# A graph and expert network on one core: the attention's ring of gathered blocks gets 32 slots in place of 25, over the place of the last stage's weights

## What is computed

```python
x = x + L0_gnn(layernorm(x))     # sum over edges of (x @ W[rel])[src] * weight, 16 relations
x = x + L0_ffn(layernorm(x))     # 16 experts, 2 for each node
x = x + L1_gnn(layernorm(x))     # two layers of graph attention, 8 heads of 32
x = x + L1_ffn(layernorm(x))     # a shared MLP and 4 gated experts

def gat_conv(x, src, dst, W, a_src, a_dst, b):
    h = (x @ W).reshape(N, HEADS, HEAD_DIM)
    alpha_s = jnp.einsum('nhc,hc->nh', h, a_src)
    alpha_d = jnp.einsum('nhc,hc->nh', h, a_dst)
    e = alpha_s[src] + alpha_d[dst]
    e = jnp.where(e > 0, e, NEG_SLOPE * e)
    m = jax.ops.segment_max(e, dst, num_segments=N)
    ex = jnp.exp(e - m[dst])
    denom = jax.ops.segment_sum(ex, dst, num_segments=N)
    alpha = ex / (denom[dst] + 1e-16)
    out = jax.ops.segment_sum(h[src] * alpha[:, :, None], dst, num_segments=N)
    return out.reshape(N, HEADS * HEAD_DIM) + b
```

## Time and profile before

| what | value |
| --- | --- |
| three runs | 3178.21, 3187.8, 3189.51 us |
| their median | 3187.8 us |
| the profiled execution's own time | 3155.48 us |
| its span in the profile | 3153.7 us |
| busy in it: PE, DVE, POOL, ACT | 62%, 49%, 44%, 29% |
| gathers of the attention, L1539 | 784, mean 1000 ns |

### The profile page before, as it was taken

One profiled execution on the slowest core, in us unless ns is written; L12 is line 12 of the kernel. 1 busy time (PEld: TensorE's weight loads), 2 busy tenths in 40 slices (PEclk: granted clock), 3 DMA queues, 4 the chain that ended last, 5 costly groups with the idle time before them and its releaser, 6 DMA issues.

```text
span 3153.7 us, 37574 instructions
## 1 busy us (share of the span) xinstructions
PE 1954.5 (62%) x10213; PEld 1541.1 (49%) x10213; DVE 1545.1 (49%) x4921; ACT 920.9 (29%) x2031; POOL 1402.8 (44%) x1413
## 2 busy tenths in 40 slices
PE   8998444354457999733554665564355465556599
PEld 6887233243337999622443443443244343344377
DVE  4200123233376555634564664675355555556753
ACT  5444667672013444320111111113011111111432
POOL 1100666666602344245555555513555555552143
PEclk9999677666778999876677666787677767776799
DMA  6544566564338999744344344313343443442000
GB/s 229 199 190 198 178 194 198 186 208 131 90 84 274 352 351 352 236 151 121 101 130 125 107 126 123 115 56 112 107 124 118 121 122 117 119 122 79 1 14 28
DMA packets 206433, 472.17 MB, mean 150 GB/s; under 512 B 33180, under 2 KB 99958, under 8 KB 199762
## 3 DMA queue, kind: packets, MB, share of 16 engines
q0 software_dynamic: 63424, 179.09, 20.0%
q1 hardware_dynamic: 111986, 188.65, 16.8%
q10 hardware_dynamic: 30816, 101.99, 9.1%
HBM read 365.49 MB, written 104.92 MB: 149 GB/s over the span
## 4 chain that ended last, share of the span: by engine, by line
PE 29%; another core or an unknown queue 29%; DVE 26%; issue 10%; DVEq 3%; DMA 2%; ACT 1%; POOL 1%; SPq 0%; ACTq 0%; POOLq 0%
PE banks L470 9%; PE banks L1332 7%; DVE arena L1737 3%; DVE arena L1821 3%; DVE arena L891 3%; PE banks L1344 3%; DVE X L900 2%; DVE arena L1786 2%; DVEq L761 2%; DVEq L764 1%; PE banks L1498 1%; PE banks L877 1%; DVE xn L1749 1%; PE banks L2240 1%
## 5 line engine op out<-in xcount | busy, mean ns | idle before, releaser
L1539 POOL DMA_INDIRECT arena<-ht,srcT x784 | 784.2, 1000 | 678.4 <-DVE arena L1821 382.1
L1648 PE MATMUL banks<-arena,XT 128*128 128x264 f32 x884 | 385.0, 527 | 281.1 <-DVE arena L1821 193.9
L849 POOL DMA_INDIRECT arena<-tr,idx1T x392 | 376.7, 961 | 362.0 <-DMA tr<-arena 175.2
L877 PE MATMUL banks<-arena 128*128 x884 | 259.9, 456 | 326.2 <-DVE arena L891 261.2
L877 PEld LDWEIGHTS banks<-arena 128*128 128x128 f32 x884 | 196.9, 231 | 389.3 <-issue 357.2
L1648 PEld LDWEIGHTS banks<-arena,XT 128*128 128x128 f32 x884 | 208.6, 255 | 347.5 <-DVE arena L1821 204.8
L1649 PE MATMUL banks<-arena,XT 128*128 128x264 f32 x884 | 352.6, 489 | 0.0
L1821 DVE TENSOR_TENSOR arena<-arena,nrmT 128x528 f32<-128x528 f32 x442 | 309.7, 703 | 20.3 <-issue 12.7
L900 DVE TENSOR_TENSOR X<-X,banks 128x256 f32 x221 | 91.8, 415 | 397.1 <-remote 368.9
L470 PE MATMUL banks<-parts 128*128 128x512 f32 x1200 | 281.0, 394 | 0.0
L1737 DVE TENSOR_TENSOR arena<-arena,banks 128x264 f32 x442 | 189.0, 428 | 136.2 <-remote 113.3
(11 more groups left out here) (381 smaller groups left out, 3268.1 us busy)
## 6 DMA issues: line engine op xcount, KB each, us to landing
arena<-in_L_ffn_w_dram SPq DMA_DIRECT2D x192, 512.0 KB
tr<-arena SPq DMA_DIRECT2D x50, 1024.0 KB, 3.9
XT<-otd ACTq DMA_DIRECT2D x52, 512.0 KB
arena<-ohd ACTq DMA_DIRECT2D x52, 512.0 KB
arena<-dld ACTq DMA_DIRECT2D x28, 512.0 KB
otd<-arena ACTq DMA_DIRECT2D x28, 512.0 KB
ohd<-arena ACTq DMA_DIRECT2D x28, 512.0 KB
arena<-ht,srcT POOLq DMA_INDIRECT x784
```

Source lines behind the costliest of these rows:

```text
L849: pool.indirect_dma_start(Gr[:, o:o + D], None, TR, bass.IndirectOffsetOnAxis(ap=idx1T[:, q:q + 1], axis=0)).then_inc(d_g[b % NG], 16)
L877: mm = ten.matmul(B[n][:, 0:D], OHr[:, n, h, :], Gr[:, h * D:][:, bass.ds(o, D)], start=(h == 0), stop=(h == 1))
L1539: pool.indirect_dma_start(Gall[:, o:o + ROW], None, HT[L], bass.IndirectOffsetOnAxis(ap=srcT[:, q:q + 1], axis=0)).then_inc(d_g[b % NG], 16)
L1648: ten.matmul(B[n][:, 0:MSG], OH[b][:, 2 * j, :], WG[:, j, 0, :], start=True, stop=False)
```

## The change

`RG` becomes 32 and the ring takes the place in which the last stage's large weights lay: these now overlap the ring's upper slots (`raw_at` is at the end of the region `parts2`), and only the small ones (biases, `B5`) keep a place at the top, over that of the first layer's weights. The table `given` starts at block 0 in place of block 3, and `NEAR` becomes 16. The 14 loads and the 4 behind them go to the end of the second attention layer: SyncE waits until all chunks but the last are weighed (`LAST_OF_RING`), and GpSimd clears the two tiles there in place of VectorE. `O`, `O2` and `hst` lie elsewhere in the arena than before; what reads and writes them is the same.

```diff
@@ -45,7 +45,7 @@
 HALF = 16
 NX = 3
 RB = 40
-RG = 25
+RG = 32
 GIVEN0 = (4 - RG) % 4
 KTH = 4096
 WHOLE = 12582912.0
@@ -823,7 +823,7 @@
 
         ld_ok = sem("ld_ok")
         landed = ten.alloc_register("landed")
-        NEAR = 20
+        NEAR = 16
         begun, starts = pool.alloc_register("begun"), [pool.alloc_register(f"start{i}") for i in range(16)]
 
         def pool_gather():
@@ -912,12 +912,20 @@
 
 
 
-        LATER = ARENA - 5600
+        LATER = ARENA - 1872
         top[0] = LATER
         wx2 = [take(2 * 272).rearrange("p (k c) -> p k c", k=2) for _ in range(2)]
         bb2 = [take(D) for _ in range(2)]
         tad = take((NS + CH) * 8)
-        raw_at = top[0]
+        top[0] = LATER
+        gB = take(4)
+        sb1 = take(2)
+        sb2 = take(1)
+        eb1 = take(4)
+        eb2 = take(2)
+        B5 = take(D)
+        assert top[0] <= LATER + 2 * 272
+        raw_at = top[0] = PARTS2_AT + PARTS2
         sW1 = take(2 * D).rearrange("p (k c) -> p k c", k=2)
         sW2 = take(2 * P).rearrange("p (k c) -> p k c", k=2)
         sW3 = take(D)
@@ -926,12 +934,6 @@
         eW3 = take(2 * D).rearrange("p (q c) -> p q c", q=2)
         gW = take(2 * 4).rearrange("p (k c) -> p k c", k=2)
         raw_end = top[0]
-        gB = take(4)
-        sb1 = take(2)
-        sb2 = take(1)
-        eb1 = take(4)
-        eb2 = take(2)
-        B5 = take(D)
 
         def by_tile(n, dt=F32, t=NT):
             return take(t * n, dt=dt).rearrange("p (t r) -> p t r", t=t)
@@ -1133,8 +1135,6 @@
                                           ALU.add).then_inc(wx_ok, 1)
                         vec.wait_ge(wx_ok, 4 * layer + 2 * k + n + 1)
             dv.put(vec.memset(tad[:, NT * 8:], 0.0))
-            vec.memset(B5[0:8, :], 0.0).then_inc(wx_ok, 1)
-            vec.memset(eW2, 0.0).then_inc(wx_ok, 1)
 
         NRUN = (NT + 3) // 4
         lgr = [v[0:R, :] for v in sil]
@@ -1236,9 +1236,6 @@
             results(MT - 1)
 
         def sp_routing():
-            def once(view, src, **kw):
-                sync.dma_start(view, src, **kw).then_inc(d_fw, 16)
-
             sync.dma_start(gw, a["L0_ffn_gate_w"].rearrange("(k p) r -> p k r", p=P)).then_inc(d_gw, 16)
             sync.dma_start(gbb, a["L0_ffn_gate_b"].rearrange("(o r) -> o r", o=1).to_broadcast([P, R])).then_inc(d_gw, 16)
             for g in range(NGR):
@@ -1253,6 +1250,19 @@
                     sync.dma_start(avb2[layer][:, n, :],
                                    v.rearrange("h c -> (h c)").rearrange("(o c) -> o c", o=1)
                                    .to_broadcast([P, D])).then_inc(d_gp, 16)
+
+        LAST_OF_RING = CH * NCH + CH * (NCH - 1)
+
+        def pool_last_rows():
+            pool.wait_ge(w_ok, LAST_OF_RING)
+            pool.memset(eW2, 0.0).then_inc(wx_ok, 1)
+            pool.memset(B5[0:8, :], 0.0).then_inc(wx_ok, 1)
+
+        def sp_last_rows():
+            def once(view, src, **kw):
+                sync.dma_start(view, src, **kw).then_inc(d_fw, 16)
+
+            sync.wait_ge(w_ok, LAST_OF_RING)
             once(sW1, a["L1_ffn_sW1"].rearrange("(k p) c -> p k c", p=P))
             once(sW2, a["L1_ffn_sW2"].rearrange("(k p) c -> p k c", p=P))
             once(sW3, a["L1_ffn_sW3"])
@@ -1267,8 +1277,6 @@
             once(eb1, a["L1_ffn_eb1"].rearrange("e p -> p e"), allow_slow_non_contiguous=True)
             for h in range(2):
                 once(eb2[64 * h:64 * h + 64], a["L1_ffn_eb2"].rearrange("(q h) p -> h p q", h=2)[h], allow_slow_non_contiguous=True)
-
-        def sp_last_rows():
             sync.wait_ge(wx_ok, 10)
             for h in range(2):
                 sync.dma_start(eW2[:, :, h, 64 * h:64 * h + 64],
@@ -1298,7 +1306,6 @@
                 sp_tile(j)
             for j in range(NW, MT):
                 sp_tile(j)
-            sp_last_rows()
 
         def sp_combine():
             sync.wait_ge(d_yg[0], 16 * ((MT + 1) // 2))
@@ -1443,19 +1450,20 @@
         TB3 = TB.rearrange("p (n c) -> p n c", c=48)
         tmid = take(CH * 8)
         O_AT = top[0]
-        Gall = take(RG * 2 * ROW + CH * 2 * MSG)
-        WG = Gall[:, RG * 2 * ROW:].rearrange("p (s a c) -> p s a c", s=CH, a=2)
+        WG = take(CH * 2 * MSG).rearrange("p (s a c) -> p s a c", s=CH, a=2)
         xtf = XT[:, :, :].rearrange("p k n -> p (k n)")
         OH = [xtf[:, i * CC * P:(i + 1) * CC * P].rearrange("p (s c) -> p s c", c=P) for i in range(2)]
         OT = [xtf[:, (4 + i) * CC * P // 2:(5 + i) * CC * P // 2].bitcast(BF16) for i in range(2)]
-        hst = Gall[:, 24 * 2 * ROW:26 * 2 * ROW].rearrange("p (b c) -> p b c", b=4)
         SB = take(CC * 13, dt=BF16).rearrange("p (s c) -> p s c", c=26)
         OHf = [take(CC * P // 2, dt=BF16) for _ in range(2)]
         OHb = [v.rearrange("p (s c) -> p s c", c=P) for v in OHf]
         vp = take(CH)
+        Gall = take(RG * 2 * ROW)
         assert top[0] <= LATER, (top[0], LATER)
-        O = [Gall[:, i * 5 * D:(i + 1) * 5 * D].rearrange("p (t c) -> p t c", c=D) for i in range(3)]
-        O2 = [Gall[:, (3 + i) * 5 * D:(4 + i) * 5 * D].rearrange("p (t c) -> p t c", c=D) for i in range(3)]
+        hst = Gall[:, 24 * 2 * ROW:26 * 2 * ROW].rearrange("p (b c) -> p b c", b=4)
+        assert raw_end <= top[0] - 2 * ROW and (ET - 5) % RG == RG - 1
+        O = [arena[:, O_AT + i * 5 * D:O_AT + (i + 1) * 5 * D].rearrange("p (t c) -> p t c", c=D) for i in range(3)]
+        O2 = [arena[:, O_AT + (3 + i) * 5 * D:O_AT + (4 + i) * 5 * D].rearrange("p (t c) -> p t c", c=D) for i in range(3)]
         LOW = NT * R + NT * 8
 
         mo_ = Offsets(vec, rm, 8, (NS - 1) * 8)
@@ -1528,7 +1536,7 @@
                     pool.wait_ge(ld_ok, ET * (L + 1) + b - 4)
                 if b % 4 == 0 and b + 3 >= RG:
                     n = (b + 4 - RG) // 4
-                    if n % 16 == 0 or b < RG:
+                    if n % 16 == 0 or b < RG + 4:
                         pool.load(firsts[n % 16:], given[0:1, n:n - n % 16 + 16])
                     pool.reg_alu(gone, firsts[n % 16], 1, ALU.max)
                     pool.reg_alu(past, gone, L * NCH * CH, ALU.add)
@@ -1559,6 +1567,8 @@
             ends_and_places(sync, L, 1)
             for b in range(ET):
                 sp_block(L + 1, b)
+            if L:
+                sp_last_rows()
 
         def act_gat(L):
             def scores(c):
@@ -2399,6 +2409,7 @@
             arrive(pool)
             meet(pool, 4)
             pool_gat(1)
+            pool_last_rows()
             arrive(pool)
             meet(pool, 5)
             pool_last_norm()
```

## The result

The changed kernel takes 3211.7 us (median of 8 runs, 3207.1 to 3217.3), the kernel before 3187.2 us in the same rounds (8 runs, 3178.2 to 3198.3). The ratio is 1.0074 [1.0057, 1.0091]: slower by 24.5 us, where 22.4 were forecast.

The account below looks back on a forecast made before the run. TensorE's signals, held while GpSimd issues gathers, were taken to bound the attention layers. Each layer: +17 for the fill, -5.8 for the chunks, +11.2; two give +22.4, other terms 0, on 3187.8: 3210 us, range 3174 to 3224.

Parts of the forecast that it names:

- What bounds the kernel: Attention layers: TensorE's signals are held while GpSimd issues gathers, costing 8 to 11 us a chunk; slot waits (382.1 us) don't bind.
- The kinds of chunks: Middle of each attention layer: chunks sorted by gathers issued and where; a ring of 32 shifts their counts, -5.8 us a layer.
- The first fill is longer: Start of each attention layer: 16 more gathers delay the first weighing, +17 us a layer, bounded by 0 and 20.2.
- The first gather stage and the late weights: First gather stage with NEAR 16, 4.4 us per pause more or less; last stage's weights loaded late, up to +3: both taken as 0.
- That gathers hold nothing: Rival for the attention layers: the longer fill is free, two layers give -11.6, 3176 us; chance 0.17.
- that half is held: Rival for the first fill: the expansion gets through in 12 us, +5.8 offsets -5.8 a layer, 3188 us; chance 0.10.
- that the slots are the bound: Rival for the attention layers: 7 more blocks remove GpSimd's slot waits, 397 us less, about 2790 us; chance 0.05.
- The fourth, more held than counted: Rival: late weights (+3), two more first-stage pauses (+8.8) or a fill costing its full 20.2 (+6.4), 3213 to 3228; chance 0.08.

Follow-up runs that it names:

- the second profile of before: The kernel before, profiled once more with no edit: 3187.3 us in a single execution, span 3185.6 us.
- the run without gathers: Changed kernel, but SyncE issues 392 plain DMAs of adjoining rows a layer in place of GpSimd's gathers: 2667.2 us, ratio 0.845; output not the reference's.
- the two places of the hold: Changed kernel, with freed groups of four blocks waiting besides until TensorE has expanded the next chunk: 3214.7 us, ratio 1.0092.
- the cut: Changed kernel, first fill 20 blocks, then 7 a chunk in pieces of 5 and 2: 2930.9 us, ratio 0.9261; all 7 in one run: 3027.8 us, 0.9608.
- the earlier trace: The first profile of the kernel before, unedited, from which the prediction was made: 3155.48 us, span 3153.7 us.

## Why the prediction came out right, and where it did not

The time (3210 forecast, 3212 measured), its sign and the place, the first fill, were right. That the sum came out within 2 us is partly luck: the fill cost 11 us more than taken, the rest of the layers gave back 3 us more, and 6 us lie ahead of the layers where I had put nothing.

- **What bounds the kernel**: right. GpSimd's wait for slots, 382.1 us, was no loss that a larger ring could lift; it is 409.6 us with 32 slots and 412.2 in the second profile of before. TensorE's signals are held while GpSimd gathers: shown by the run without gathers, by the two places of the hold, and by the cut. That it is the issuing, and not another part of a gather, stays argued.
- **The kinds of chunks**: right in their count and order; -5.8 us a layer forecast, -5.4 and -8.9 measured against the second profile of before. The first one, from which the durations came, was a quick execution, so 684 in place of 695 us a layer. Since both kernels shift alike, the difference was not touched.
- **The first fill is longer**: this is the term that was mis-sized. +17 us a layer, with 20.2 as its upper bound; measured 22.9 and 22.3. The bound took the distance from the fill's end to the expansion as fixed. The 16 gathers are 20.0 us, and that distance grew as well: 7.0, 8.8 and 9.9 us behind 48, 56 and 64 gathers in the first layer, 6.8, 7.9 and 9.1 in the second. Two layers make it 11 us more than I took.
- **The first gather stage and the late weights**: 0, as taken. The run with 25 slots, `NEAR` = 20 and all else of the change gives 0.9997. The first gather stage has 17 waits and 74.4 us where 16 were counted (16 and 70.9 in the earlier trace rows), within the 4.4 us that a pause more was to cost.
- Sum of the two profiles: 22.9 - 5.4 + 22.3 - 8.9 = +30.9 in the layers, -6.0 ahead of them, together +24.9 by parts, +24.8 in the spans (3210.4 - 3185.6). The medians of 8 runs each differ by 24.5 too, so the chance of one execution doesn't explain the 6.0 away: how the 24.5 of the medians divide into parts no run here shows.
- **The rivals.** That gathers hold nothing (3176) and that half is held (3188) fall with the first weighing at 93.4 us; that the slots are the bound (2790) falls with GpSimd's wait, which stayed, and with the unchanged kinds of chunks. The fourth, more held than counted, came true in its part on the fill, whose price it put at 20.2.

What stays open: why the chip holds TensorE's signals while GpSimd issues; why the distance behind a long fill is 7 to 10 us and behind a run of 10 or 16 only 1.5 to 2.7; why the maxima come at 53.2 to 54.6 us in fills of 40 to 64, which is some 3 us behind the end of the one of 40; why a run of 14 or 16 holds to its end in some chunks and not in others. No run here separates GpSimd's making of the descriptors from anything else that it does for a gather, nor scattered rows from rows that lie together: plain DMAs from GpSimd, and scattered rows issued by SyncE, were not tried.

## What to carry to other kernels

A deeper ring buys nothing where its consumer sets the pace, and it is filled once at the start: ask first what the fill holds up. Where long runs of gathers from GpSimd stand beside a chain through TensorE, look at what ends VectorE's waits, and put the gathers in short pieces that end before the next signal of the chain is due; here 5 and 2 blocks a chunk at two signals took 7% off, and 4 and 3 only 3%. Take the durations and the time from executions of one group of runs: two profiles of the same kernel differed by 1% here, more than the change.

## What the runs showed of the hardware

- While GpSimd issued gathers without a pause, what waited for TensorE often went on only 2.1 to 2.7 us after the end of a run of 14 or 16, 1.5 us after one of 10, and 7 to 10 us after a fill of 48 to 64. In other chunks it was let go 2 to 6 us before the end of such a run, or 0.4 us before it in the earlier trace rows. The maxima got through inside a fill of 48, 56 or 64, 53.3 to 54.6 us after its start; with fills of 32 and 40 they came some 5 and 3 us after the fill's end, 45.1 and 53.2 us after its start.
- The same number of bytes by plain DMAs from SyncE, of rows that lie together, held nothing: chunks of 17.2 to 18.8 us at 163 GB/s, against 26.6 to 29.7 with 16 gathers, at 109 over the layer.
- Beside runs of gathers TensorE's rows can end long before what waits for them goes on: 27 us in the first fill (1435.70 and 1462.68), 12 us in a chunk (1671.41 and 1683.67). Those ends are modelled.
- The kernel before had medians of 3157.5, 3158.6, 3189.2 and 3201.1 us in the four groups of runs. Between the two profiles of it the difference lies for the most part in the chunks with 16 gathers, 25.54 against 26.66 us for one kind, while those without were alike (17.7 to 18.2 against 16.9 to 18.4).
